# Slot tiles of two sizes in a routed expert layer

## The reference, cut to what matters

```python
weights = softmax(x @ gate_w.T + expert_bias)
top_w, top_i = top_k(weights, 2); top_w = top_w / (sum(top_w) + 1e-6)
for e in range(8):
    h = gelu(x @ w_up[e].T)          # 256 -> 1024 features
    y = h @ w_down[e].T              # 1024 -> 256
    out = out + sparse_w[..., e:e+1] * y
out = layernorm(out) + x
```

## Time and profile before

| | us |
|---|---|
| median of 3 runs (range) | 823.22 (821.9 to 823.74) |
| profiled execution | 824.23 |
| its span, first to last instruction | 822.4 |
| TensorE matmul busy | 720.0 (88%) |
| VectorE busy | 536.5 (65%) |
| GpSimd busy | 441.4 (54%) |
| ScalarE busy | 363.5 (44%) |
| mean granted TensorE clock | 0.932 |

### The profile page before, as it was taken

The page is one execution under the profiler, slowest core; times in us unless marked ns, Lnnn a source line. Parts: engine busy times, 40 slices in busy tenths (PEclk is TensorE's granted clock), DMA queues, the critical chain, the costliest instruction groups (busy, mean ns, idle before and its releaser), DMA issues.

```text
span 822.4 us, 20968 instructions
## 1 busy us (share of the span) xinstructions
PE 720.0 (88%) x6400; PEld 648.0 (79%) x6401; DVE 536.5 (65%) x1182; ACT 363.5 (44%) x657; POOL 441.4 (54%) x584
## 2 busy tenths in 40 slices
PE   4999999999999718599999999999999999999200
PEld 4999999999999514498899999998899898998100
DVE  4889888888888579455555555555555555554295
ACT  2877777777777403122222222222222222222184
POOL 3777787788787407524444444344443444422287
PEclk9999999999999855699999999999999999999655
DMA  4333333333332100111111111111111111110594
GB/s 157 109 108 121 104 121 103 120 104 119 103 121 85 41 7 0 54 38 53 53 51 47 44 49 45 45 51 51 51 51 45 45 51 45 45 38 27 171 304 164
DMA packets 39875, 64.54 MB, mean 78 GB/s; under 512 B 5408, under 2 KB 30240, under 8 KB 39840
## 3 DMA queue, kind: packets, MB, share of 16 engines
q1 hardware_dynamic: 31632, 42.37, 16.0%
q0 software_dynamic: 7488, 20.46, 7.7%
q10 hardware_dynamic: 720, 1.26, 0.5%
HBM read 45.46 MB, written 18.61 MB: 78 GB/s over the span
## 4 chain that ended last, share of the span: by engine, by line
PE 87%; DVE 4%; issue 3%; DMA 2%; POOL 2%; ACT 1%; SPq 0%; ACTq 0%; DVEq 0%; POOLq 0%
PE ps_a L530 25%; PE ps_b L544 25%; PE ps_b L433 7%; PE ps_a L391 4%; PE ps_b L400 4%; PE ps_c L412 4%; PE ps_c L417 3%; PE ps_a L468 3%; PE ps_a L455 2%; PE ps_c L498 2%; PE ps_c L514 2%; PE ps_a L479 1%; PE ps_c L378 1%; PE ps_a L443 1%; DMA w_hi<-y_rows 1%
## 5 line engine op out<-in xcount | busy, mean ns | idle before, releaser
L530 PE MATMUL ps_a<-area,w_hi 128*128 128x256 f16 x1248 | 207.7, 274 | 1.7 <-DVE area L795 1.7
L544 PE MATMUL ps_b<-w_hi,area 128*128 x1248 | 206.4, 273 | 0.0
L1055 POOL DMA_INDIRECT y_rows<-area x78 | 77.9, 999 | 209.4 <-ACT area L940 197.5
L530 PE MATMUL ps_a<-area,w_lo 128*128 128x256 f16 x624 | 170.7, 274 | 0.0
L544 PE MATMUL ps_b<-w_lo,area 128*128 x624 | 170.1, 273 | 0.0
L935 ACT ACTIVATE area<-ps_a 128x512 f32<-128x512 f32 x156 | 93.1, 597 | 142.0 <-PE ps_a L530 142.0
L530 PEld LDWEIGHTS ps_a<-area,w_hi 128*128 x1248 | 122.3, 98 | 16.1 <-issue 2.1
L544 PEld LDWEIGHTS ps_b<-w_hi,area 128*128 128x128 f16 x1248 | 122.1, 98 | 14.1
L793 DVE TENSOR_SCALAR area<-ps_c 128x512 f16<-128x512 f32 x39 | 27.0, 691 | 151.7 <-PE ps_c L514 151.7
L805 DVE SCALAR_TENSOR_TENSOR area<-area 128x512 f16<-128x512 f32 x156 | 108.3, 694 | 5.4
L940 ACT ACTIVATE area<-ps_b 128x512 f32<-128x512 f32 x39 | 23.3, 597 | 181.1 <-PE ps_b L544 181.1
(11 more groups left out here) (129 smaller groups left out, 1250.2 us busy)
## 6 DMA issues: line engine op xcount, KB each, us to landing
area<-weights SPq DMA_DIRECT2D x32, 512.0 KB, 3.3
w_hi<-y_rows SPq DMA_DIRECT2D x32, 256.0 KB, 4.0
resid<-x_in SPq DMA_DIRECT2D x32, 128.0 KB, 2.1
area<-ctx_t SPq DMA_DIRECT2D x32, 128.0 KB, 2.1
xn_rows<-area SPq DMA_DIRECT2D x32, 128.0 KB, 1.7
out<-w_lo SPq DMA_DIRECT2D x16, 256.0 KB, 2.6
area<-xn_rows,area POOLq DMA_INDIRECT x78, 2.8
y_rows<-area POOLq DMA_INDIRECT x78
```

Of the source, the lines that this page charges most:

```text
L530: mm = pe.matmul(ps_h[:, q, (ic % 2) * SLOTS:(ic % 2 + 1) * SLOTS], w[:, bass.ds(first + (hc * I + ic * P), P)], r[b][:, hc, :], start=(n ...
L544: mm = pe.matmul(ps_y[:, b, v * D:(v + 1) * D], g[b][:, ic, v * P:(v + 1) * P], w[:, bass.ds(first + (EXPERT_COLS + ic * D), D)], start=(n ...
L1055: pool.indirect_dma_start(y_rows[:, :], bass.IndirectOffsetOnAxis(ap=didx[b][:, v:v + 1], axis=0), y_s[b][:, v * D:(v + 1) * D], None).the ...
```

## The change

The 39 slot tiles stay 39, but only the first 32 (`PAIR_TILES`) have two units. The last seven (`ONE_TILES`) have one unit of 128 slots, so there are 71 units in place of 78. Every expert's slots are now rounded up to whole units. The chain of VectorE instructions shares the tiles out: an expert gets its full pairs of units in the two-unit tiles as long as these last, and the rest of its units in the one-unit tiles. In the expert stage every operation on a tile k of 32 or above works on one unit: `up` has as many matmuls but 128 moving columns, `down` has half the matmuls, there are two transposes in place of four, and the vector, scalar and gather/scatter work is halved. The loop now covers steps 4 to 27 (`MOE_LAST` = 28) and the rest is unrolled. The diff, cut to its core:

```diff
-SLOT_TILES = TOKENS * TOPK // SLOTS + E - 1
-UNITS = SUBS * SLOT_TILES
+PAIR_TILES = TOKENS * TOPK // SLOTS
+ONE_TILES = E - 1
+SLOT_TILES = PAIR_TILES + ONE_TILES
+UNITS = SUBS * PAIR_TILES + ONE_TILES
...
-    r[:, R_STEP:R_STEP + TILES] = (SLOTS * np.arange(TILES))[None]
+    r[:, R_STEP:R_STEP + TILES] = (P * np.arange(TILES))[None]
...
-        MOE_FIRST, MOE_LAST = 4, 36
+        MOE_FIRST, MOE_LAST = 4, PAIR_TILES - 4
+        def subs(k):
+            return SUBS if not isinstance(k, int) or k < PAIR_TILES else 1
...
-                    for v in range(SUBS):
+                    for v in range(subs(k)):
                         at = c * SLOTS + v * P
                         mm = pe.transpose(ps_x[:, b, at:at + P], xg[b][:, v, c * P:(c + 1) * P], ident)
...
-                            mm = pe.matmul(ps_h[:, q, (ic % 2) * SLOTS:(ic % 2 + 1) * SLOTS],
-                                           w[:, bass.ds(first + (hc * I + ic * P), P)], r[b][:, hc, :],
+                            cols = subs(k) * P
+                            mm = pe.matmul(ps_h[:, q, (ic % 2) * cols:(ic % 2 + 1) * cols],
+                                           w[:, bass.ds(first + (hc * I + ic * P), P)], r[b][:, hc, 0:cols],
                                            start=(n == 0), stop=(n == 3 * HC - 1))
...
-                for v in range(SUBS):
+                for v in range(subs(k)):
                     n = 0
                     for ic in range(IC):
...
-            link(dve.tensor_reduce(tiles_e, eq, AX.X, ALU.add))
-            link(dve.tensor_tensor_scan(tin, rc[:, R_ONES:R_ONES + E], tiles_e, 0.0, ALU.mult, ALU.add))
-            link(dve.tensor_tensor(tex, tin, tiles_e, ALU.subtract))
-            link(dve.scalar_tensor_tensor(base, tex.unsqueeze(2).to_broadcast([P, E, TILES]), float(SLOTS), base, ALU.mult, ALU.add))
-            link(dve.tensor_tensor(flat(pos), ps_b[:, 0, 0:E * TILES], flat(base), ALU.add))
+            dve.tensor_tensor(flat(pos), ps_b[:, 0, 0:E * TILES], flat(base), ALU.add).then_inc(rt_rank, 1)
+            link(dve.tensor_reduce(units_e, eq, AX.X, ALU.add))
+            link(dve.tensor_reduce(pairs_e, eq[:, :, 1:TILES:2], AX.X, ALU.add))
+            link(dve.tensor_tensor_scan(tin, rc[:, R_ONES:R_ONES + E], pairs_e, 0.0, ALU.mult, ALU.add))
+            link(dve.scalar_tensor_tensor(odd_0[:, 0:1], pairs_e[:, 0:1], -float(SUBS), units_e[:, 0:1], ALU.mult, ALU.add))
+            link(dve.scalar_tensor_tensor(odd_0[:, 0:1], tin[:, E - 1:E], float(PAIR_TILES), odd_0[:, 0:1], ALU.is_lt, ALU.mult))
+            link(dve.tensor_tensor(pairs_e[:, 0:1], pairs_e[:, 0:1], odd_0[:, 0:1], ALU.add))
+            link(dve.tensor_scalar(tin, tin, odd_0[:, 0:1], None, ALU.add))
+            link(dve.tensor_tensor(tex, tin, pairs_e, ALU.subtract))
+            link(dve.tensor_scalar(tex, tex, float(PAIR_TILES), float(SLOTS), ALU.min, ALU.mult))
+            link(dve.tensor_scalar(tin, tin, float(PAIR_TILES), float(SLOTS), ALU.min, ALU.mult))
+            link(dve.tensor_tensor(full_rows, tin, tex, ALU.subtract))
+            link(dve.scalar_tensor_tensor(left_e, full_rows, -1.0 / P, units_e, ALU.mult, ALU.add))
+            link(dve.tensor_scalar(left_e, left_e, 0.0, None, ALU.max))
+            link(dve.tensor_tensor_scan(rin, rc[:, R_ONES:R_ONES + E], left_e, 0.0, ALU.mult, ALU.add))
+            link(dve.tensor_tensor(rex, rin, left_e, ALU.subtract))
+            link(dve.scalar_tensor_tensor(shift_e, rex, float(P), tin, ALU.mult, ALU.subtract))
+            link(dve.tensor_scalar(shift_e, shift_e, float(PAIR_TILES * SLOTS), None, ALU.add))
+            dve.wait_ge(rt_rank, 1)
+            link(dve.tensor_tensor(eq, pos, full_rows.unsqueeze(2).to_broadcast([P, E, TILES]), ALU.is_ge))
+            link(dve.tensor_tensor(eq, eq, shift_e.unsqueeze(2).to_broadcast([P, E, TILES]), ALU.mult))
+            link(dve.tensor_tensor(base, pos, tex.unsqueeze(2).to_broadcast([P, E, TILES]), ALU.add))
+            link(dve.tensor_tensor(flat(pos), flat(base), flat(eq), ALU.add))
...
+            link(dve.tensor_scalar(tex, tex, 1.0 / SLOTS, None, ALU.mult))
+            for ends, n_tiles, at_k in ((tex, PAIR_TILES, 0), (rex, ONE_TILES, PAIR_TILES)):
+                link(dve.tensor_tensor(ecmp[:, 0:n_tiles, :], ends[:, 1:E].unsqueeze(1).to_broadcast([P, n_tiles, E - 1]),
+                                       rc[:, R_IOTA:R_IOTA + n_tiles].unsqueeze(2).to_broadcast([P, n_tiles, E - 1]), ALU.is_le))
+                link(dve.tensor_reduce(ecount[:, at_k:at_k + n_tiles], ecmp[:, 0:n_tiles, :], AX.X, ALU.add))
...
-                        act.activation(g_s[q], ps_h[:, q, :], ACT.Gelu, scale=1.0 / (X_SCALE * W_SCALE)).then_inc(g_r, 1)
+                        n = 2 * subs(k) * P
+                        act.activation(g_s[q][:, 0:n], ps_h[:, q, 0:n], ACT.Gelu, scale=1.0 / (X_SCALE * W_SCALE)).then_inc(g_r, 1)
...
-                    for v in range(SUBS):
+                    for v in range(subs(k)):
                         pool.indirect_dma_start(y_rows[:, :], bass.IndirectOffsetOnAxis(ap=didx[b][:, v:v + 1], axis=0),
```

More of the change, by code:

```diff
@@ L157, in program @@
         lmax, lsum, lrec, m1, m2, i1, i2, den, drec = (carve(TILES) for _ in range(9))
-        tiles_e, tin, tex = carve(E), carve(E), carve(E)
+        units_e, pairs_e, odd_0, tin, tex, left_e, rin, rex, full_rows, shift_e = (carve(E) for _ in range(10))
         pos_j = carve(TOPK * TILES)
@@ L164, in program @@
         tile_val = [carve(RG * 2 * UNITS, F16).rearrange("p (v s g) -> p v s g", g=RG, v=2) for _ in range(2)]
[L165 removed]
+        ecmp = carve(PAIR_TILES * (E - 1)).rearrange("p (k e) -> p k e", e=E - 1)
         ecount = carve(SLOT_TILES)
@@ L266, in program @@
         rt_cnt = sem("rt_cnt")
-        rt_slot = sem("rt_slot")
+        rt_slot, rt_rank = sem("rt_slot"), sem("rt_rank")
         rt_grp = sem("rt_grp")
@@ L284, in program, with unit, moved, moved_before @@
             sem(n) for n in ("c_f0", "c_f1", "c_stats", "c_mvr", "c_ver", "c_rsr", "c_nmr", "c_ap", "c_out"))
-        MOE_FIRST, MOE_LAST = 4, 36
+        MOE_FIRST, MOE_LAST = 4, PAIR_TILES - 4
+        def subs(k):
+            return SUBS if not isinstance(k, int) or k < PAIR_TILES else 1
+        def unit(k):
+            return SUBS * k if subs(k) == SUBS else SUBS * PAIR_TILES + k - PAIR_TILES
+        def moved(k, half):
+            return 16 * SUBS * (half + 1) if subs(k) == SUBS else 16 * (SUBS * PAIR_TILES // 2 + (k - PAIR_TILES) // 2 + 1)
+        def moved_before(k, half):
+            return 16 * SUBS * half if subs(k) == SUBS else moved(k, half) - 16
         def moe_steps(eng, lo, step):
@@ L338, in _ @@
             steps(sp, 0, step)
-            sp.wait_ge(scat[0], 16 * SUBS * ((SLOT_TILES + 1) // 2))
-            sp.wait_ge(scat[1], 16 * SUBS * (SLOT_TILES // 2))
+            sp.wait_ge(scat[0], moved(SLOT_TILES - 1, 0))
+            sp.wait_ge(scat[1], moved(SLOT_TILES - 2, 0))
             sp.wait_ge(y_ps, SLOT_TILES)
@@ L508, in transpose_rows @@
             def transpose_rows(k, half, b):
-                pe.wait_ge(gat[b], 16 * SUBS * (half + 1))
+                pe.wait_ge(gat[b], moved(k, half))
                 since(pe, xl_r, k - 1)
                 for c in range(HC):
-                    for v in range(SUBS):
+                    for v in range(subs(k)):
                         at = c * SLOTS + v * P
@@ L791, in moe @@
                     since(dve, h_ps, GQ * (k - 1))
-                    src = ps_x[:, b, :].rearrange("p (c n) -> p c n", c=HC)
-                    dve.tensor_scalar(xt_hi[b], src, X_SCALE, None, ALU.mult).then_inc(xh_r, 1)
+                    n = subs(k) * P
+                    src = ps_x[:, b, :].rearrange("p (c n) -> p c n", c=HC)[:, :, 0:n]
+                    dve.tensor_scalar(xt_hi[b][:, :, 0:n], src, X_SCALE, None, ALU.mult).then_inc(xh_r, 1)
                     dve.wait_ge(xh_r, k + 1)
-                    dve.scalar_tensor_tensor(xt_lo[b], src, X_SCALE, xt_hi[b], ALU.mult, ALU.subtract).then_inc(xl_r, 1)
+                    dve.scalar_tensor_tensor(xt_lo[b][:, :, 0:n], src, X_SCALE, xt_hi[b][:, :, 0:n], ALU.mult, ALU.subtract).then_inc(xl_r, 1)
                 k, half, b = here(j, u, 1)
@@ L798, in moe @@
                     since(dve, y_ps, k - 1)
+                    n = subs(k) * P
                     for q in range(GQ):
                         c = slice(q * IC // GQ, (q + 1) * IC // GQ)
-                        src = g_s[q].rearrange("p (c n) -> p c n", n=SLOTS)
+                        src = g_s[q][:, 0:2 * n].rearrange("p (c n) -> p c n", n=n)
                         dve.wait_ge(g_r, GQ * k + 1 + q)
-                        dve.tensor_scalar(g_hi[b][:, c, :], src, G_SCALE, None, ALU.mult).then_inc(gh_r, 1)
+                        dve.tensor_scalar(g_hi[b][:, c, 0:n], src, G_SCALE, None, ALU.mult).then_inc(gh_r, 1)
                         dve.wait_ge(gh_r, GQ * k + 1 + q)
```

(17 more changed lines are left out.)

3 lines of the change are left out of this document (removed).

## The result

The median is 799.04 us (797.57 to 800.66, 4 runs) against 823.35 (821.9 to 823.74, 4 runs): a ratio of 0.971, 95% interval 0.9685 to 0.9732. The forecast was 799.7, with 791 to 806 as its range. The profiled execution took 799.62 us with a span of 797.8.

The account below looks back on a forecast made before the run. TensorE's stream was taken to bound the expert stage, 10.92 us a tile. Expert stage -25.0, routing chain +4.3, routing loop -1.3 and end -1.5 gave -23.5 us on 824.23: 800.7, median 799.7, range 791 to 806.

Parts of the forecast that it names:

- The bound of a short tile: One-unit expert tiles: TensorE's instruction stream, 7.66 us a tile, exceeds the array's 5.48 and becomes the bound.
- The 244 ns a group: Sequencer's time per address group of three `up` matmuls, or 81 ns a matmul; expected throughout a short tile.
- One sign: Trace after, short tiles: TensorE's gaps put down to issue, the longest where the expert number is read.
- Rival A: Short-tile `up`: columns decide, not the sequencer; 55 ns a matmul, median 786.6 us; chance 9%.
- Rival B: Short-tile `up`: the weight load decides, 107 to 109 ns a matmul, only `down` gains; median 804.8 us; chance 14%.
- The expert stage: Steps 30 to 38 of the expert stage: 92.2 us become 67.2, saving 25.0 us.
- The routing: Before the expert stage: longer chain of dependent links +4.3 us net, routing loop -1.3 us.
- the loop: Routing loop: 71 units for 78 save 0.16 us a round, -1.3 us with narrower last matmuls; between 0 and -1.8.
- The expert table: End of routing: three more small instructions, some 0.6 us, hidden by 1.65 us of cover; free.
- The end: Behind the last expert matmul: one scatter goes and the copy of y narrows, -1.5 us.
- Rival C: Short tiles: TensorE waits for instructions and the clock falls; median near 831 us, or no change; chance 5%.
- Rival D: Short tiles: a late gather or semaphore makes the period 9 us, 10 us less gain, about 809; chance 4%.

Follow-up runs that it names:

- fixed addresses: The kernel after, with the seven one-unit tiles taking expert 0's weights at build-time addresses (result partly wrong): 785.8 us, ratio 0.955 to the kernel before.
- The chain alone: The kernel before, plus 12 chained instructions of 8 elements and 4 of 256 per pair, results unchanged: 827.35 us against 822.44.
- One reading: The kernel after, with a one-unit tile's expert number read once and its register kept for `down`: 793.15 us, ratio 0.964 to the kernel before.
- wide `up`: The kernel after, with `up` of one-unit tiles moving 256 columns again (result partly wrong): 802.47 us, ratio 0.975 to the kernel before.
- apart: The kernel after, with the seven one-unit tiles at positions 0, 2, 4, 32, 34, 36, 38, between two-unit tiles: 791.71 us.
- both: The kernel after, with one-unit tiles between two-unit tiles and, outside the loop, the expert number read once a tile: 788.02 us.

## Why the prediction was right

**The bound of a short tile** was the step that decided, and it held. The 244 ns a group read from before came out at 247 in step 33, the period of 7.66 at 7.68 to 7.80. The remaining tenth is made of single groups with longer gaps, which I had averaged from too few: over steps 33 to 38, unrounded in the trace, most gaps are 237 ns, a little over a quarter are 250 to 390, and the mean is 254. One sign didn't come as written: I expected TensorE's gaps to be put down to issue, and in the matmuls' row 3.4 us are put down to VectorE (only the loads' row says issue, 5.4 us). The longest gap of step 33, 0.88 us from 706.93 to 707.81, does lie where the expert number is read ahead of `down`. Ahead of `up` there is almost none, because `down` runs at 109 ns a matmul, and the sequencer gets ahead meanwhile.

Rival A is refuted as to the kernel, but its 55 ns are what the array can do: 56 ns in the start of step 32, and throughout with fixed addresses. Rival B is refuted: the f16 matmuls start 56 ns apart, each with its own load of 128 columns, so these loads don't hold the matmuls 107 ns apart, though the record of each is 95 to 99 ns long. Taken as the interval from one load to the next, the Trainium skill's figure, "TensorE: Matmul & The Clock Gate", section "LDWEIGHTS (loading the stationary operand)", doesn't hold for these f16 loads; where page and measurement differ, the measurement decides.

**The expert stage** gave 23.2 us where 25.0 were forecast. From the first transposes of step 30 to the copy of the last y are 92.33 us before (673.28 to 765.61) and 68.33 after (676.06 to 744.39): 24.0 saved, so 1.0 us is missing there. It comes from the longer period, from step 31 (9.32 against 9.13) and from the start of the row of short tiles. The other 0.8 is a term that I had left out, the clock at the start of the stage. Before, the array ran at 0.50 from the first `up` matmul at 338.56 until about 341.7, 3.2 us; after, from 340.51 until about 345.4, 4.9 us, and half of the additional 1.7 is lost. The last section shows that single executions of the same code differ as much.

**The routing** was forecast at +4.3 and -1.3, and measured at +4.26 and, for the loop, 20.73 to 19.19 = -1.5. The expert table was free, as forecast, but with less to spare: its first added instruction, of 8 elements, took 1.25 us beside GpSimd's last L1069, and the cover left is 0.84 us, not 1.

**The end** gave its -1.5. The last stage's -1.9 was not forecast, and neither was the attention's -0.7. The attention's is scatter: the eight traces of this document have 297.4 to 299.2 us up to the counts, with no changed instruction in them. So is 0.8 of the last stage: from its first load to the end of the last store's issue are 47.9 us before and 47.1 after, and 46.7 to 48.1 in the other six. The other 1.1 is real. Behind the last store's issue the two traces with the old tiles have 3.8 us, the six with the new ones 2.7. GpSimd closes the kernel with a DRAIN, and that is what got shorter (before, then after; count, ns min/median/max, first and last start):

```profile
L76 POOLq DRAIN  x1: 5312/5312/5312, 816.9 to 816.9; - x1
L78 POOLq DRAIN  x1: 4164/4164/4164, 793.4 to 793.4; - x1
```

The chain alone, with the old tiles, has 5308 ns; the other five, with the new ones, have 4161 to 4168. GpSimd issues 14 indirect DMAs fewer with the new tiles (142 in place of 156); that this is the reason is not tested.

**How near the total came is in part luck.** The median missed the forecast by 0.7 us, but the expert stage gave 1.8 less than forecast, and 2.6 came from stretches where I had counted nothing, 1.1 of them real and 1.5 scatter.

**Rival C** didn't come: the clock stayed at 1.00 through the short steps, with TensorE starved every 7.7 us. **Rival D** neither: no gather was waited for in them.

## What to carry to other kernels

Before halving a dimension, read the spacing of the register instructions between the matmuls in a stretch where the queue isn't full: that is the issue rate, and once the array is faster than it, columns are free and instructions are what counts. Busy time doesn't show it, since the records overlap. Where short work must be done, put it beside long work, whose surplus of issue time pays for it, and keep in a register what is read twice.

## What the runs showed that I had not expected

The moment at which the full clock is granted at the start of the expert stage differs from one execution to the next. A window of the fixed-address run and one of the kernel after, both from about the first `up` matmul to the rise (start:end, length, busy PE, PEld, DVE, ACT, POOL, clock, DMA share, GB/s):

```profile
339.80:342.85 3.05, 3.05 (x15) 2.29 (x16) 0.00 (x0) 0.22 (x1) 1.49 (x2) 0.50 0.31 87
340.50:345.30 4.80, 4.79 (x23) 3.64 (x24) 1.12 (x2) 0.60 (x1) 1.74 (x4) 0.50 0.20 58
```

With fixed addresses the low clock ends 3.1 us behind the first `up` matmul, after 4.9. One reading and wide `up` have 4.2 each. These four run the same instructions up to step 30. Before and the chain alone have 3.2 and 5.0, apart 6.2, both 3.1. So the 1.7 us between before and after are within what one and the same stretch of code shows, and nothing here shows that the 0.8 that they cost the expert stage is a price of the longer routing. Stages of two single traces can therefore not be compared here to better than about a microsecond.

A wait's releaser in the profile can be an engine that was done long ago. The 3.4 us put down to VectorE went away when a reading of TensorE's own stream was removed.

The end of the kernel depends on GpSimd's work too: its closing DRAIN was 1.1 us shorter in every trace with the new tiles, although the last stage itself is unchanged.
